# Four-layer GNN and attention network on one core: a sixth region of expert weights in the place of the edge counts and masks

## What is computed

```python
logits = jnp.einsum('bmd,dnp->bmnp', xn, phin)          # 625 tokens x 64 slots
d = jax.nn.softmax(logits, axis=1)                      # over tokens
c = jax.nn.softmax(logits.reshape(b_, m_, n_ * p_), axis=-1).reshape(b_, m_, n_, p_)
xs = jnp.einsum('bmd,bmnp->bnpd', xn, d)                # one row of 768 for each slot
h = gelu(jnp.einsum('bnpd,ndh->bnph', xs, w1) + b1)     # w1: 64 x 768 x 192
ys = jnp.einsum('bnph,nhd->bnpd', h, w2) + b2           # w2: 64 x 192 x 768
y = jnp.einsum('bnpd,bmnp->bmd', ys, c)
```

## Time and profile before

| | |
|---|---|
| runs | 2966.78, 2961.51, 2971.74 us; median 2966.78 us |
| profiled execution | span 2958.9 us from first to last instruction; its device time is not listed by itself, the fastest run is 2.6 us longer than the span, the median 7.9 us |
| PE busy | 2721.0 us, 92% of the span |
| DVE, ACT, POOL busy | 1415.1, 1128.2, 704.2 us |
| granted TensorE clock | 0.972 of full speed in the mean |
| transfers | 220.37 MB, 74 GB/s in the mean |
| slot experts | 64 transfers of 576 KB and 48 of 768 KB, 75.5 MB |

### The profile page before, as it was taken

The page is one execution under the profiler, slowest core; times in us unless marked ns, Lnnn a source line. Parts: engine busy times, 40 slices in busy tenths (PEclk is TensorE's granted clock), DMA queues, the critical chain, the costliest instruction groups (busy, mean ns, idle before and its releaser), DMA issues.

```text
span 2958.9 us, 48747 instructions
## 1 busy us (share of the span) xinstructions
PE 2721.0 (92%) x20003; PEld 2472.4 (84%) x20003; DVE 1415.1 (48%) x3609; ACT 1128.2 (38%) x2106; POOL 704.2 (24%) x260
## 2 busy tenths in 40 slices
PE   8999999997769999998999899989997999999797
PEld 8999999994339878998888899989676888795697
DVE  8777565573122135568733632231665564105632
ACT  6633265551003213329431342232654243445231
POOL 0134311110002412220334143324112341103121
PEclk9999999998799999999999999999999999999899
DMA  2022221017981112220121122212001121100121
GB/s 69 12 76 79 86 71 38 30 46 280 414 333 57 59 33 55 65 83 26 44 69 50 60 65 76 76 54 76 17 9 52 54 81 49 36 22 23 33 65 59
DMA packets 163790, 220.37 MB, mean 74 GB/s; under 512 B 21521, under 2 KB 142795, under 8 KB 163570
## 3 DMA queue, kind: packets, MB, share of 16 engines
q1 hardware_dynamic: 163570, 217.26, 22.1%
HBM read 215.31 MB, written 1.92 MB: 73 GB/s over the span
## 4 chain that ended last, share of the span: by engine, by line
PE 58%; DVE 7%; ACT 3%; DMA 2%; issue 2%; POOL 1%; SPq 0%; DVEq 0%; ACTq 0%; POOLq 0%
PE ps L58 41%; PE ps L1968 3%; DMA expert_regions<-in_L_ffn_w 2%; PE ps L1882 2%; PE ps L2134 1%; PE ps L2272 1%; PE ps L2155 1%; PE ps L690 1%; PE ps L609 1%; PE ps L599 1%; ACT buf L1079 1%; PE ps L698 1%; DVE buf L2011 1%; DVE buf L2020 1%; PE ps L2916 1%
## 5 line engine op out<-in xcount | busy, mean ns | idle before, releaser
L58 PE MATMUL ps<-weights_r,buf_r 128*125 128x256 f32 (+3 forms) x4050 | 538.6, 284 | 5.7 <-POOL weights_r L276 1.9
L276 POOL TENSOR_TENSOR weights_r<-weights,weights_r 128x1536 fp32r<-128x1536 f32 (+1 forms) x79 | 273.6, 3463 | 1042.8 <-ACT weights_r L269 1029.4
L58 PEld LDWEIGHTS ps<-weights_r,buf_r 128*125 128x125 f32 (+1 forms) x4050 | 508.1, 186 | 9.0 <-issue 4.2
L276 POOL TENSOR_TENSOR weights_r<-weights,head_weights_r 128x1536 fp32r<-128x1536 f32 (+1 forms) x77 | 270.3, 3510 | 1021.7 <-ACT head_weights_r L269 1013.2
L58 PE MATMUL ps<-xT_r,weights_r 128*128 128x376 f32 (+1 forms) x2100 | 345.4, 310 | 0.0
L58 PEld LDWEIGHTS ps<-xT_r,weights_r 128*128 128x128 f32 x2100 | 313.4, 188 | 4.8 <-issue 2.8
L58 PE MATMUL ps<-head_weights_r,buf_r 128*125 128x256 f32 (+2 forms) x2310 | 316.1, 283 | 0.0
L58 PEld LDWEIGHTS ps<-head_weights_r,buf_r 128*125 128x125 f32 x2310 | 293.3, 187 | 0.0
L58 PE MATMUL ps<-weights_r,xT_r 128*125 128x256 f32 x1680 | 233.3, 282 | 8.0 <-issue 4.8
L269 ACT ACTIVATE head_weights_r<-weights 128x1536 fp32r<-128x1536 f32 (+1 forms) x77 | 112.8, 1465 | 306.1 <-PE ps L58 193.1
L58 PEld LDWEIGHTS ps<-weights_r,xT_r 128*125 128x125 f32 x1680 | 212.8, 186 | 10.3 <-issue 5.4
(11 more groups left out here) (368 smaller groups left out, 4310.2 us busy)
## 6 DMA issues: line engine op xcount, KB each, us to landing
expert_regions<-in_L_ffn_w SPq DMA_DIRECT2D x64, 576.0 KB, 15.3
expert_regions<-in_L_ffn_w SPq DMA_DIRECT2D x48, 768.0 KB, 20.5
weights<-in_L_mix_fc_w SPq DMA_DIRECT2D x24, 768.0 KB, 4.5
weights<-in_L_gnn_W SPq DMA_DIRECT2D x18, 768.0 KB, 4.6
weights<-in_L_ffn_W SPq DMA_DIRECT2D x12, 768.0 KB, 4.7
weights<-in_L_mix_w_mapT SPq DMA_DIRECT2D x9, 768.0 KB, 4.8
weights<-in_L_gnn_W_out SPq DMA_DIRECT2D x9, 768.0 KB, 4.5
weights<-in_L_mix_kqv_wT SPq DMA_DIRECT2D x9, 768.0 KB, 4.6
```

The lines of the kernel that those rows point to most:

```text
L58: mm = net.nc.tensor.matmul(ps, net.r(stationary(s, k)), net.r(moving(m, k)), start=(n == 0 and k == 0), stop=(stop and n == 2 and k == kc ...
L276: self.nc.gpsimd.tensor_tensor(self.r(load.dst), load.dst, self.r(load.high), ALU.subtract).then_inc(self.low_made, 1)
```

## The change

The edge matrices move into the arena of regions as a new buffer `edges` (12,512 + 6,272 bytes for each partition), on which a sixth region lies. Before it is overwritten, SP stores the counts to DRAM (`KeepCounts`), and region 5 is filled when the last attention of layer 0 is done (`attended`) and the store has landed. After `SlotSecond` the counts are loaded back; `Degrees` waits for them on DVE. The mask is not kept: `SelfLoops` of layer 1 makes it anew, as before.

```diff
-        sizes = dict(xT=BUF, ..., weights=(WSLOTS + 1) * SLOT)
+        sizes = dict(xT=BUF, ..., weights=(WSLOTS + 1) * SLOT, edges=NT * N + 3 + 1568)
...
+ [blocks(1152, ("edges", 0, 4))]     # added to expert_blocks; blocks(1536, ("edges", 0, 3)) to tile_blocks
...
+        self.counts = nc.alloc_sbuf_tensor_at("edge_counts", [128, NT, N], F32, offset=at - 4 * sizes["edges"])
+        self.mask = nc.alloc_sbuf_tensor_at("edge_mask", [128, NT, N], BF16, offset=at - 4 * sizes["edges"] + 4 * (NT * N + 3))
+        self.counts_kept, self.kept = nc.dram_tensor("counts_kept", (TP, NT * N), F32, kind="Internal").ap(), sem("counts_kept_landed")
-        self.counts = sb("edge_counts", [128, NT, N])
-        self.mask = sb("edge_mask", [128, NT, N], BF16)
...
+class KeepCounts:
+    def __init__(self, net, made):
+        self.net, self.made = net, made
+        self.before, self.used_at = self, (len(net.stages) - 1, 1 << 20)
+        net.loads.append(self)
+
+    def sync(self, sp):
+        for sem, value in self.made:
+            sp.wait_ge(sem, value)
+        sp.dma_start(self.net.counts_kept, self.net.counts[:TP].rearrange("p t n -> p (t n)")).then_inc(self.net.kept, 16)
...
-    EXPERTS, GROUP, DEPTH, TILES = 64, 4, 5, 3
+    EXPERTS, GROUP, DEPTH, TILES = 64, 4, 6, 3
...
 class Degrees(Stage):
     def vector(self, dve):
         self.begin(dve)
+        self.landed(dve)
         done = self.net.dve
         self.nc.vector.tensor_reduce(self.rdeg, self.net.counts[:TP], AX.X, ALU.add).then_inc(done.sem, done.one())
...
     bias_out = CopyRow(net, tok(G[5]), net.row(ins["L0_gnn_b_out"]))
+    KeepCounts(net, loops.ends())
     for i in range(3):
         attended = rest().ends()
...
             units = linear_units(net, ins["L0_gnn_W_out"], tok(G[5]), "add", tok(G[5]), (i * D, (i + 1) * D))
+            FirstFetches(net, ins["L0_ffn_w1"], (5,), attended + [(net.kept, 16)])
             norm = LinearReluNorm(...)
...
-    SlotSecond(...)
+    second = SlotSecond(...)
...
-    degrees = Degrees(net, rdeg)
+    counts = net.into(net.counts[:TP].rearrange("p t n -> p (t n)"), net.counts_kept, second.ends())
+    degrees = Degrees(net, rdeg, counts)
```

More of the change, by code:

```diff
@@ L109, in __init__ @@
         self.ps = ctx.enter_context(nc.psum_tensor("ps", [128, BANKS, 512], F32))
-        sizes = dict(xT=BUF, **{f"buf{i}": BUF for i in range(6)}, head_weights1=NT * N + 3, weights=(WSLOTS + 1) * SLOT)
+        sizes = dict(xT=BUF, **{f"buf{i}": BUF for i in range(6)}, head_weights1=NT * N + 3, weights=(WSLOTS + 1) * SLOT, edges=NT * N + 3 + 1568)
         at, plain, self.rounded = -(-nc.sbuf_base // 32) * 32, {}, {}
@@ L118, in __init__ @@
         parts = [("buf1", "buf3", 0), ("buf4", "buf3", 1536)]
-        self.expert_blocks = [blocks(1152, (*q, 4)) for q in whole] + [blocks(1152, (a, 0, 3), (b, o, 1)) for a, b, o in parts]
-        self.tile_blocks = [blocks(1536, (*q, 3)) for q in whole] + [blocks(1536, (a, 0, 2), (b, o, 1)) for a, b, o in parts]
+        self.expert_blocks = [blocks(1152, (*q, 4)) for q in whole] + [blocks(1152, (a, 0, 3), (b, o, 1)) for a, b, o in parts] + [blocks(1152, ("edges", 0, 4))]
+        self.tile_blocks = [blocks(1536, (*q, 3)) for q in whole] + [blocks(1536, (a, 0, 2), (b, o, 1)) for a, b, o in parts] + [blocks(1536, ("edges", 0, 3))]
         for name, n in sizes.items():
@@ L156, in __init__ @@
         self.sem = sem
-        self.esem = [sem(f"experts_landed{j}") for j in range(5)]
+        self.esem = [sem(f"experts_landed{j}") for j in range(SlotExperts.DEPTH)]
         self.freed, self.nbank = {}, 0
@@ L3141, with __init__ @@
     side = True
-    def __init__(self, net, rdeg, after=None):
+    def __init__(self, net, rdeg, counts, after=None):
         super().__init__(net, after)
-        self.rdeg = rdeg
+        self.rdeg, self.loads = rdeg, [counts]
         self.take(dve=2, act=1)
@@ L3555, in network @@
     SlotHidden(net, wide.rearrange("p (c h) -> p c h", c=2), hidT)
-    SlotSecond(net, hidT, ins["L0_ffn_w2"], offsets, [masked2[:, k * 384:(k + 1) * 384].rearrange("p (t c n) -> p t c n", t=3, c=2) for k in range(2)],
+    second = SlotSecond(net, hidT, ins["L0_ffn_w2"], offsets, [masked2[:, k * 384:(k + 1) * 384].rearrange("p (t c n) -> p t c n", t=3, c=2) for k in range(2)],
                rows2, ys[:, 0:HALF], first, now() + offs.ends())
@@ L3789, in _ @@
             for load in sorted(net.loads, key=lambda q: q.before.used_at if q.before else (-1, 0)):
-                if isinstance(load, (SlotExperts, FirstFetches)):
+                if isinstance(load, (SlotExperts, FirstFetches, KeepCounts)):
                     load.sync(sp)
```

## The result

The changed kernel takes 2973.82 us (median of 15 runs, 2968.50 to 2978.45), the kernel before 2964.49 us (15 runs, 2957.39 to 2971.74). The ratio is 1.0031, with a 95% interval of 1.0023 to 1.0038: 9.3 us slower (7 to 11), just above the 0.3% (8.9 us) that the prediction took as the least that it could tell. The interval leaves out 1, so the kernel is slower, if only by a little. The profiled execution took 2971.34 us, with a span of 2969.6 us.

What follows compares the result with a forecast made beforehand. PE was taken as the bound (92% busy), except from 720 to about 868 us, where weight bytes at the DMA rate bound. -5.7 + 9.0 + 1.3 = +4.6 us on 2966.8 gave 2971.4 us, range 2961 to 2978.

Steps and rivals of the forecast that it cites:

- Part 1, the sixth region: Weight stream of SlotFirst and SlotSecond: one refill fewer after turn 0, last turn one interval earlier, -5.7 us.
- Part 2, the store: Store of the counts at about 415 us, in idle time of SP's queue: costs 0.
- Part 3: Load of the counts after SlotSecond and DVE's wait: landing 14.0 us after issue, +10.3 us in all.
- behind the counts on the engines that carry them: Fourth weight unit's fetch queues behind the counts until about 917.7, lands by 922.3, covered by ACT's own 6 us delay.
- Issue of the counts: In SP's list behind five small loads after LinearNorm: issued at 905.10, before subtracting the stream's gain.
- From landing to the third unit: Chain over DVE, ACT and POOL from the counts' landing to the third weight unit being split: 11.3 us.
- PE's gap: PE stands ahead of the first LinearT's third weight unit, ready at 930.4 instead of 921.4: 9.0 us.
- The clock: After PE's gap, half speed for 2.7 us: costs 1.3 us, bounds 0 and 2.7.
- the case of 16 engines: Rival: counts load over 16 engines, landing at 910.9, PE stands 0.8 us; -4.9 us, 2961.9 us; chance 0.17.
- Long rows: Rival: the counts' 12,500-byte rows load below 130 GB/s; at half rate +16.6 us, 2983.4 us; chance 0.12.
- That the gain does not come: Rival: refills paced by something other than bytes with six regions, leaving +10.3 us, 2977.1 us; chance 0.06.
- The 5.6 us: Counts' load time by the skill's fit, 2.0 us plus bytes at 436 GB/s: landing at 910.7, gain about 5 us.

Runs made afterwards that it cites:

- experiment 2: Changed kernel with the counts' load early in SP's list, five regions and no first fetch of region 5: 2963.07 us against 2961.74 of the kernel before, ratio 1.0004.
- Experiment 6: Changed kernel with SP waiting for the counts to land before its next weight fetch: 2970.90 us against 2962.85 of the kernel before, ratio 1.0026.
- Experiment 7: Changed kernel with six products of zeros on PE in the gap before the third weight unit: 2973.17 us against 2964.45 of the kernel before, ratio 1.0029.
- experiment 1: Changed kernel with the counts' load moved ahead of the five small loads in SP's list: 2959.03 us against 2961.74 of the kernel before, ratio 0.9985.
- experiment 3: Changed kernel with row sums taken early on DVE, only Apply waiting for the counts' load: 2958.57 us against 2961.74 of the kernel before, ratio 0.9987.
- experiment 8: Changed kernel with the load cut into 112 and 13 partitions and 2,500-byte rows in DRAM: 2967.44 us against 2964.45 of the kernel before, ratio 1.0016.
- experiment 4: Changed kernel with the counts' load cut into 112 and 13 partitions, same place in SP's list: 2968.43 us against 2961.74 of the kernel before, ratio 1.0019.
- experiment 5: Kernel before, five regions, plus only the counts' store, load back and DVE's wait: 2979.30 us against 2962.85 of the kernel before, ratio 1.0050.

## Why the prediction was right, and where it was off

The forecast was 4.6 us more than before (2971.4 us), called no change, with the gain of the stream given back at the wait. 9.3 us were measured, twice as much, with an interval of 7 to 11 us around the 0.3% bound: "no change" was right by little. The time of 2973.82 us is nearer to the forecast than the difference is, and that is luck: the forecast started from 2966.78, a median of three runs, and the longer series of the kernel before has 2964.49. The chain was right link by link; two terms of it were too small, the length of the load (and with it the gap) and the clock. Together they are 2.6 us, which makes 7.2, the low end of the interval.

- **Part 1, the sixth region, -5.7 us: right.** The stream is 5.8 us shorter in the changed kernel (151.6 against 157.4), and experiment 2 without the region is back at 157.1. The profile shows 4.75 at the last turn because the refills started 1.06 us later, and the start scatters by 4.9 us.
- **Part 2, the store, 0: right.** It was issued at 414.52, and experiment 2 is level with the kernel before.
- **Part 3, landing 14.0 us after issue: too small, 16.05.** The step "behind the counts on the engines that carry them" was right for the weight fetch, which landed 11.8 us after its issue, but took the load itself as undisturbed. While the fetch ran on the eleven other engines, the packets of the counts took 0.83 us instead of 0.47 (910 to 913 against 904 to 907). Experiment 6 without the fetch has 14.46. The five engines at 130 GB/s, taken from the output store, were right.
- **Issue of the counts.** Forecast at 905.10 less the gain, 899.4; it was 901.02. Of the 1.6 us, 0.9 is the smaller shift (the small loads began 4.8 us earlier, not 5.7) and 0.6 the small loads (4.06 us instead of 3.43; 3.29 to 4.06 over the runs).
- **From landing to the third unit, 11.3 us: right**, 924.68 + 3.43 - 917.07 = 11.04.
- **PE's gap, 9.0 us: 10.6.** The load was 2.05 us longer and the small loads ahead of it 0.7; against that, the chain behind was 0.3 shorter and PE itself came 0.8 later, from its slower first unit.
- **The clock, 1.3 us: 2.3.** I took the 2.7 us at half speed from one return to dense work. Behind the gap the granted clock stayed at 0.50 for about 5 us. Experiment 7 shows that it is the clock; why it stayed low longer is not shown. The return used as a model had short products before it, and in the changed kernel that same return cost 0.8 us more than before as well.

In the profile: -4.75 at the last turn, +0.84 for the first unit's first 18 products (5.23 instead of 4.39 us: 894.50 to 899.73 against 899.30 to 903.69), 10.6 for the gap and 2.3 for the clock are 9.0 us; the first 18 products of the third unit end 9.1 us later (933.61 against 924.51). The other 1.6 us of the 10.7 in span come later: between two activation table loads of ACT in layer 1 are 45.4 us (1121.02 to 1166.40) where the kernel before has 43.8. The granted clock from 1152 to 1162 was 0.83 there, 1.00 before. The same 45.4 stand in experiment 1 and 43.8 in experiment 3, both without the gap, so the gap is not needed for it. Of the six traces with a gap five have 1.5 to 2.7 us more at this place, of the four changed kernels without one only experiment 1: whether the gap makes it more frequent stays open.

The rivals: the case of 16 engines is excluded by the trace (share 0.3 for most of the transfer). Long rows are no brake on five engines: 14.46 us alone, 0.4 more than worked out for rows of 3 KB. That the gain does not come is refuted by experiments 1 and 2. The 5.6 us that the prediction takes from the Trainium skill ("DMA: Bandwidth & Descriptors", section "Anatomy of one DMA") were not met: 14.46 us were measured for the load alone and 10.5 when it was spread over all engines. That section gives its fit for transfers issued by GpSimd, and SP issued this one.

## What to carry to other kernels

A transfer that makes room for a prefetch has to be paid where it comes back: look first at what stands ahead of it in the issuing engine's list, then at who is queued behind its waiter, for a side result that is first read 134 us later (917.07 to 1051.56) held up the splitting of weights here. Take the price of a transfer from a row with the same number of partitions, not of the same size; 125 partitions used 5 of 16 DMA engines. And a PE gap cost its length plus 1.8 to 2.6 us for the slow start after it here.

## What the runs showed of the hardware that had not been expected

- A gap of 3.7, 5.3, 9.2 or 10.6 us ahead of the same 18 products (experiments 8, 4, 6, the changed kernel) made them take 5.5, 5.7, 5.5 and 5.4 us instead of 3.1. In experiment 5, with 10.9 us, they took 4.9. In each of these traces the granted clock was 0.50 when PE returned. The slow start was not cheaper for the shorter gaps, so shortening a gap saves less than it seems until it is closed.
- A transfer on five engines was slowed by another on the eleven others: the 768 KB fetch issued 6.2 us behind the counts lengthened the counts' landing by 1.6 us (experiment 6 without it: 14.46; with it 16.05, in experiments 5 and 7 16.04 and 15.83), their packets taking 0.83 us instead of 0.47. On the five engines the fetch's packets came behind those of the counts.
- Reading the stored counts back on 16 engines ran at 200 to 340 GB/s with the share at 1.0, where the expert weights have 418. Row length was tried and is not the main cause, and the weight fetch's packets began only when 124 of the 125 long rows had. Whether it is the reading back of DRAM that was written from 5 engines, or something else in where the tensor lies, was not tried and stays open.
